# Making the one-hot tiles of a graph network's second edge pass on VectorE instead of ScalarE

## The reference, cut to what matters

```python
h = jax.nn.silu(edge_scalars @ (Wfc1 / jnp.sqrt(jnp.float32(FC_IN))))
w = h @ (Wfc2 / jnp.sqrt(jnp.float32(FC_H)))            # w0, w1, w2, w3
...
e0 = f0[edge_src]                                       # 64 scalars of the source node
e1 = f1[edge_src]                                       # 32 vectors of the source node
mid0 = w0 * e0 * sh0
mid1 = w3 * jnp.einsum('eum,em->eu', e1, sh1) / jnp.sqrt(3.0)
mid2 = w1[:, :, None] * e0[:, :, None] * sh1[:, None, :]
mid3 = w2[:, :, None] * e1 * sh0[:, :, None]
cnt = jnp.clip(jax.ops.segment_sum(jnp.ones(edge_dst.shape, x.dtype), edge_dst, num_segments=n), 1.0)

def smean(v):
    s = jax.ops.segment_sum(v, edge_dst, num_segments=n)
    return s / cnt.reshape((n,) + (1,) * (v.ndim - 1))
```

## Time and profile before

| | |
|---|---|
| Median of 3 runs | 9516.46 us (9511.68 to 9518.3) |
| The profiled execution's own time | 9520.71 us |
| Its span, first to last instruction | 9518.9 us |
| Mean granted clock of TensorE | 0.907 of full speed |
| PE busy | 7548.9 us, 79% |
| DVE busy | 7566.5 us, 79% |
| ACT busy | 4696.1 us, 49% |
| POOL busy | 5817.6 us, 61% |

### The profile page before, as it was taken

The page is one execution under the profiler, slowest core; times in us unless marked ns, Lnnn a source line. Parts: engine busy times, 40 slices in busy tenths (PEclk is TensorE's granted clock), DMA queues, the critical chain, the costliest instruction groups (busy, mean ns, idle before and its releaser), DMA issues. The chain is left out here.

```text
span 9518.9 us, 200533 instructions
## 1 busy us (share of the span) xinstructions
PE 7548.9 (79%) x44896; PEld 5782.9 (61%) x44896; DVE 7566.5 (79%) x19181; ACT 4696.1 (49%) x13345; POOL 5817.6 (61%) x5814
## 2 busy tenths in 40 slices
PE   0968888888888888888888466679788888888888
PEld 0457777777777777777777355555444444444457
DVE  2469999999999999999998767653467778888865
ACT  2335555555555555555555000013477788888852
POOL 0067676766776766776764599950277777766620
PEclk9979999999999999999999799985699999999975
DMA  5344333333333333333332588882344444444433
GB/s 224 89 77 96 93 93 93 94 93 93 93 94 93 94 94 93 93 94 92 94 93 74 124 210 209 209 149 73 79 117 119 121 124 125 122 119 117 115 108 102
DMA packets 1232621, 1068.41 MB, mean 112 GB/s; under 512 B 436318, under 2 KB 1099742, under 8 KB 1231454
## 3 DMA queue, kind: packets, MB, share of 16 engines
q0 software_dynamic: 225792, 385.65, 17.1%
q1 hardware_dynamic: 702000, 406.55, 16.9%
q10 hardware_dynamic: 304784, 275.69, 8.8%
HBM read 718.54 MB, written 348.68 MB: 112 GB/s over the span
## 5 line engine op out<-in xcount | busy, mean ns | idle before, releaser
L675 POOL DMA_INDIRECT e_g_src<-table_src,e_idx x1568 | 1650.4, 1053 | 920.1 <-DVE e_vy L893 475.6
L1656 POOL DMA_INDIRECT f_e<-table,f_src x1568 | 1600.8, 1021 | 539.8 <-issue 426.7
L675 POOL DMA_INDIRECT e_g_dst<-table_dst,e_idx x1568 | 1597.7, 1019 | 477.6 <-issue 469.7
L1709 PE MATMUL f_ps_a<-f_q,f_onehot 128*128 128x384 f32 x3936 | 1443.1, 511 | 105.3 <-DVE f_q L1794 102.7
L795 ACT ACTIVATE e_m1t<-e_ps_t 128x512 f32<-128x512 f32 (+1 forms) x1176 | 700.3, 596 | 811.1 <-PE e_ps_t L712 642.9
L1709 PEld LDWEIGHTS f_ps_a<-f_q,f_onehot 128*128 128x128 f32 x3936 | 725.7, 194 | 584.1 <-DVE f_q L1794 120.7
L735 PE MATMUL e_ps_v<-e_w_gate,e_m1t 96*128 96x36 f32 x3136 | 588.8, 272 | 462.5 <-ACT e_m1t L795 462.5
L1260 PE MATMUL r_ps<-r_h,r_onehot 128*128 128x165 f32 x3936 | 682.2, 315 | 321.4 <-POOL r_h L1218 157.3
L1260 PEld LDWEIGHTS r_ps<-r_h,r_onehot 128*128 128x128 f32 x3936 | 564.8, 190 | 438.9 <-POOL r_h L1218 174.3
L735 PEld LDWEIGHTS e_ps_v<-e_w_gate,e_m1t 96*128 96x128 f32 x3136 | 475.7, 191 | 554.0 <-issue 542.5
L765 PE MATMUL e_ps_h<-e_w_h,e_m2t 128*128 128x64 f32 x3136 | 585.3, 268 | 275.0 <-ACT e_h L829 275.0
(11 more groups left out here) (270 smaller groups left out, 19170.2 us busy)
## 6 DMA issues: line engine op xcount, KB each, us to landing
r_h<-edge_values SPq DMA_DIRECT2D x492, 328.0 KB, 4.4
edge_values<-e_h ACTq DMA_DIRECT2D x392, 328.0 KB
sums<-f_acc ACTq DMA_DIRECT2D x492, 192.0 KB
f_rbf<-basis SPq DMA_DIRECT2D x492, 96.0 KB
sums<-r_acc ACTq DMA_DIRECT2D x492, 82.5 KB, 3.5
basis<-b_part SPq DMA_DIRECT2D x48, 784.0 KB, 6.7
e_rbf<-basis SPq DMA_DIRECT2D x392, 96.0 KB
e_g_src<-table_src,e_idx POOLq DMA_INDIRECT x1568
```

The costliest lines, as they stand in the source:

```text
L675: pool.indirect_dma_start(out=into[:, r, t, :], out_offset=None, in_=table, in_offset=bass.IndirectOffsetOnAxis(ap=idx[:, r, c:c + 1], axi ...
L1656: pool.indirect_dma_start(out=rows_of_units[:, place * T + t, :], out_offset=None, in_=table, in_offset=bass.IndirectOffsetOnAxis(ap=src[: ...
L1709: last = nc.tensor.matmul(ps_a[slot][:, 0:ACC1], onehot[:, r, t, :], q[:, r, t, :], start=t == 0, stop=t == T - 1)
```

## The change

`hots` moves from ScalarE to VectorE and becomes one instruction over all four tiles: (destination minus `b128`) compared for equality with the column number, read from `dst` as integers. ScalarE's six instructions go, and with them the tiles `rel` and `apart` and the semaphore `near`. VectorE makes the tiles of step s+1 at the head of step s. ScalarE's queue then goes straight from the silu to the store. `y` and `dst` share one semaphore, so that ScalarE's `take_weights` and VectorE's products wait for both loads; SP's load of `dst` waits for `hot` instead of `near`.

```diff
-        rel = sb("rel", [P, 2, T])
-        apart = sb("apart", [P, 2, T, P])
...
-        dst_in, y_in, rbf_in, stored = (ring_sem(n, RING) for n in ("dst_in", "y_in", "rbf_in", "stored"))
+        attrs_in, rbf_in, stored = (ring_sem(n, RING) for n in ("attrs_in", "rbf_in", "stored"))
...
-                sp.dma_start(y[:, r], y_d[unit]).then_inc(y_in[r], 16)
-                wait(sp, near, (s - (RING - 1)) * 2)
-                sp.dma_start(dst[:, r, :], idx_d[unit][:, T:2 * T]).then_inc(dst_in[r], 16)
+                sp.dma_start(y[:, r], y_d[unit]).then_inc(attrs_in[r], 16)
+                wait(sp, hot, s - (RING - 1))
+                sp.dma_start(dst[:, r, :], idx_d[unit][:, T:2 * T]).then_inc(attrs_in[r], 16)
...
-                act.wait_ge(y_in[r], (i + 1) * 16)
+                act.wait_ge(attrs_in[r], (i + 1) * 32)
...
-            def hots(s, r, i):
-                if not present(s):
-                    return
-                act.wait_ge(dst_in[r], (i + 1) * 16)
-                wait(act, hot, s - 1)
-                nc.scalar.activation(rel[:, r % 2, :], dst[:, r, :], ACT.Identity, bias=b128[:, bass.ds(s, 1)],
-                                     scale=-1.0).then_inc(near, 1)
-                act.wait_ge(near, s * 2 + 1)
-                for t in range(T):
-                    last = nc.scalar.activation(apart[:, r % 2, t, :], iota[:], ACT.Abs,
-                                                bias=rel[:, r % 2, t:t + 1])
-                last.then_inc(near, 1)
-                wait(act, multiplied, s - (RING - 1))
-                act.wait_ge(near, s * 2 + 2)
-                nc.scalar.activation(onehot[:, r], apart[:, r % 2], ACT.Relu, bias=1.0, scale=-1.0).then_inc(hot, 1)
...
-                hots(s + 2, *ahead(r, i, 2))
...
-            for s in range(2):
-                hots(s, s, 0)
...
+            def hots(s, r, i):
+                if not present(s):
+                    return
+                dve.wait_ge(attrs_in[r], (i + 1) * 32)
+                wait(dve, multiplied, s - (RING - 1))
+                nc.vector.scalar_tensor_tensor(onehot[:, r], bc(dst[:, r, :], 2, P), b128[:, bass.ds(s, 1)],
+                                               bc(iota[:], 1, T), ALU.subtract, ALU.is_equal).then_inc(hot, 1)
...
-                dve.wait_ge(y_in[r], (i + 1) * 16)
+                dve.wait_ge(attrs_in[r], (i + 1) * 32)
...
             def body(s, r, i):
+                hots(s + 1, *ahead(r, i, 1))
                 products(s, r, i, lambda: add(s - 2, *ahead(r, i, -2)))
 
+            hots(0, 0, 0)
             rounds(dve, body)
```

More of the change, by code:

```diff
@@ L1589, in edges1 @@
         issued = sem("issued")
-        near = sem("near")
         PRODUCT = 8
```

## The result

The changed kernel takes 9619.42 us (median of 4 runs, 9615.49 to 9634.5) against 9514.36 us (9511.68 to 9518.3) for the kernel before: 1.0113 times as long, 95% interval 1.0095 to 1.0131. The forecast was 9432 with a range to 9480, so it had the wrong sign. The profiled execution has a span of 9617.9 us.

What follows compares the result with a forecast made beforehand. GpSimd's gathers were taken to bound the first half of the loop and ScalarE the part after 8230. Gains of 70, 10, 4 and 0 us, together 84, gave 9432 us as a median, with a range from 9400 to 9480.

Steps and rivals of the forecast that it cites:

- What bounds the kernel: Changed loop: GpSimd gathers set the step until 8230, then ScalarE at 4.61 us; VectorE close at 3.94 us.
- Its waits moved as said and it became idle: ScalarE's round falls from about 4.6 to 2.3 us; waits of f_acc and f_ps_w should go.
- The price of the one-hot: VectorE's new instruction takes 0.74 us, including about 60 ns for the moving scalar; step becomes 4.27 us.
- The waits that it adds: One-hot's waits for next step's loads and earlier sums, on VectorE's queue: judged free, two whole steps left for landing.
- The rival that it costs 1.09 us: One-hot costs its other-pass mean, step 4.62 us, no gain: 9516 us; chance 0.08.
- the gathers were priced at 1.40 to 1.42 us apart: GpSimd's gather spacing in the first half, taken to stay the same after the change.
- Before 7660: nothing: First stretch of the loop: 0 us gain, VectorE's added 0.33 us absorbed by 112 landing waits of 1.8 us.
- my own bound: Stated test: a gather mean above 1.05 us would prove the forecast wrong; expected to stay near 1.02 us.
- +10, +4 and 0 us of gain before 8230: Gains by stretch: 10 us from 8040 to 8230, 4 us from 7660 to 8040, nothing before 7660.
- the 70 us after it: Gain after 8230: 206 steps falling from 4.61 to 4.27 us each.
- the one-hot blocks the gathers: Rival: each one-hot delays GpSimd by its 0.69 us, costing 169 us in the first half: 9601 us; chance 0.06.
- The pause of 0.25 us that I counted as a gain: VectorE's idle time before f_ey, waiting for the last product's semaphore; the one-hot was to fill this hole.

Runs made afterwards that it cites:

- e8: Changed kernel without making the one-hot tiles (set to zero once), so ScalarE's relief alone: 9424.3 us, ratio 0.9892 to the kernel before.
- e3: Changed kernel with ScalarE making the distances and VectorE one plain fp32 is_equal; at granted clock 0.71, ratio 1.0158 to the kernel before.
- e10: Changed kernel with the one-hot's column numbers read from PSUM and f_ey waiting for the one-hot's completion: 9567.2 us, ratio 1.0042 to the kernel before.
- e5: Changed kernel with one wait added, f_ey waiting for the one-hot's own completion: 9568.3 us, ratio 1.0041 to the kernel before.
- e9: Kernel before, with f_ey waiting for one product less and f_we for the last, removing the pause: 9719.6 us, ratio 1.0210.
- e13: Changed kernel with f_we waiting for f_ey's completion: 9538.8 us, ratio 1.0016 to the kernel before.
- e14: Changed kernel with the last product waiting for the one ahead of it: 9563.7 us, ratio 1.0041 to the kernel before.
- e6: Changed kernel with f_acc moved from behind the second f_q to right behind f_we: 9827.4 us, ratio 1.0311 to the kernel before.
- e4: Kernel before plus a spare one-hot instruction on VectorE each step, output unused; at granted clock 0.71, ratio 0.9595 to the kernel before.
- e11: Changed kernel with the one-hot's column numbers read from PSUM, no pause added: 9661.2 us, ratio 1.0142 to the kernel before.

## Why the prediction was wrong

**What bounds the kernel: right, with one gap.** GpSimd until 8230, ScalarE after it, VectorE close: the traces bear it out. The gap is that I put the end of GpSimd's rule at 8230, from a count of gathers per step. e8 shows that without ScalarE's part the step is 4.14 us on average after 8230 and not VectorE's own: GpSimd still bound a part of it (45.5 us of f_ey's waits).

**ScalarE: right.** Its waits moved as said and it became idle; worth 103 us by e8.

**The price of the one-hot: right.** 0.74 us predicted, 741 ns measured at the median. The intervals too: f_q to one-hot 7285.72 to 7286.58, one-hot to f_ey 0.66, and a step in which VectorE is not held takes 7286.58 - 7282.31 = 4.27 us, the predicted figure. Of its terms one was a little large: e3's plain is_equal of this size takes 692 ns at the median, so the form costs 49 ns and not 60. The waits that it adds cost 8.8 us at start-up and nothing else. The rival that it costs 1.09 us falls.

**The step that failed: the gathers were priced at 1.40 to 1.42 us apart, unchanged.** "Before 7660: nothing, as VectorE's added 0.33 us goes into its wait for landings" rests on that. VectorE did have the room. But the overlap was not free: what fills VectorE's idle time takes from GpSimd time in which a gather starts unhindered (717 starts, now 449), and the lost pause adds the long holds. The mean went from 1.021 to 1.186 us, and up to 8230, where the gathers set the pace, from 1.027 to 1.137. By my own bound, a gather mean above 1.05 us proves the forecast wrong. The terms: +10, +4 and 0 us of gain before 8230 were -98; the 70 us after it were 206 x (4.61 - 4.65) = -8, as GpSimd bounds that stretch too now. Together they make 106 us of loss, for the 99 by which the spans differ.

**The rival "the one-hot blocks the gathers" had the right place and nearly the right time (9601), with the wrong mechanism.** It let the one-hot hold a gather for its own 0.69 us, 169 us in the first half. By my count over the trace the 132 gathers that start in a one-hot lose 41 us in all, so that its sum came within 19 us of the result is luck. e10 removes that part from e5, and the time does not move. A large part of the cost is that VectorE's row has no pause left (e9: 2.1% with no one-hot on VectorE; e5, e13, e14: with one pause the long holds go, and 0.7 to 1.0% of the time). I gave it 0.06 because the products "already run beside the gathers" and the median was 948 ns. That was the wrong row to lean on: the mean of 1.02 against a least of 942, which I did quote as speaking for it, was the trace of the same effect, and it would have been worth holding the gathers against VectorE's instructions one by one before putting a chance on it. The pause of 0.25 us that I counted as a gain was what kept them short of the long holds.

The Trainium skill (SBUF — State Buffer, section SBUF: two separate sides) says that a VectorE operation with two SBUF inputs and a GpSimd operation that reads SBUF lock each other out for a whole instruction. I took a gather to be outside it because it reads little, and wrote that the trace agreed. It did not: in the trace of the kernel before, 290 gathers start in the product of 768 elements and lose 64 us. These runs put the gather inside the rule: it is held until the product ends, and not held by a one-hot that has one input in PSUM (e10, 62 starts). That it is the reading of its indices that meets the lock is my guess, not shown. The same section says of a VectorE instruction in a 2-port mode that GpSimd cannot write descriptors while it runs. The short holds look like that, here with plain fp32 products. The long ones fit neither statement: they pass over four and more ends of instructions, 7287.78 to 7289.26.

**What stays open.** Shown is that taking the pause away gives long holds, and that one wait per step for the instruction directly ahead removes nearly all of them (e5, e9, e13, e14). Not shown is why. Idle time in the step as such does not do it: in 52 of the 127 long holds of e9 the step had begun with f_ey waiting for its gather, and so had 90 of the 93 in e6 that start in the f_q of 384. Nor is it shown what picks the instruction in which a held gather starts: f_we in the changed kernel, the second f_dot and the f_q behind it in e6, the last product in e9. How the loss divides between the long holds and the fuller row is open too. The profile has no record of what GpSimd does inside a gather.

## What to carry to other kernels

A gap in an engine that is not the bound can be the opening through which a slower neighbour gets its work done: before filling it, hold the neighbour's instructions, one by one, against what the filled engine was doing when they started, and look at their mean over their shortest. Where GpSimd's indirect DMAs set the pace, look for long gathers as soon as VectorE's row of instructions with two SBUF operands has no pause left, and try one wait per step for the instruction directly ahead; waits for results further back, as the changed kernel has too, leave no pause. When work is moved off an engine, try the smallest part that shortens its round first: here 4 elements gave -0.39%, all of it +1.1%.

## What the runs showed of the hardware

- An indirect gather of 128 rows holds GpSimd 946 ns beside an idle VectorE or one that has one of its two tensor inputs in PSUM, and up to 1.75 us if it starts in a product of 768 elements with both inputs in SBUF (the kernel before).
- With VectorE's pause gone, it can be held over several instructions: 2.37 us in the changed kernel, 3.31 in e9, 4.23 at the most in e4.
- Taking a wait of 0.25 us from VectorE cost 2.1% (e9); adding one to the changed kernel brought its ratio to the kernel before from 1.0113 to 1.0016 (e13).
- One-hot tiles of 4 x 128 columns by scalar_tensor_tensor with an integer input and a scalar at a moving address take 741 ns, with the column numbers in SBUF or in PSUM (e11); a plain fp32 is_equal of that size takes 692 (e3).
